# The last stage of a four-layer graph network: overlapped steps, one joined turn for sums and edge sums, norms and stores by chunk

## The chip, the cores and the metric

The kernel runs on one core of one Trainium2 chip. The metric is the device time of one launch, in microseconds (us). Three launches of the kernel before took 26902.59, 26913.0 and 26931.47 us; the median is 26913.0 us.

## What is computed

The reference applies four layers to a graph with 12500 nodes of 64 features and 400000 edges. The fourth layer, with the edge sum taken over the edges that leave a node, is where the change lies:

```python
# h is the normed and rectified x, of 12500 x 64
msg = h[j] + (edge_attr @ We + be)                # 400000 edges, edge_attr of 16 features
agg = segment_sum(msg, i, 12500)
t = (1.0 + eps) * h + agg
out = relu(t @ W1 + b1) @ W2 + b2
out = (out - mean(out)) * rsqrt(var(out) + 1e-5) * gamma + beta     # over the 64 features
x = x + out                                       # the result
```

The edge weights We and their bias be are the same for all edges. So the kernel sums, for each node, the gathered h (64 columns), the number of edges (1 column) and the raw edge attributes (16 columns), and multiplies the last 17 columns by the rows be and We only afterwards.

## The kernel before

All node data lie in SBUF as 98 blocks of 128 nodes: node 128 b + p is on partition p, and block b is 64 columns wide (81 in `acc2`, which holds the sums: 64 of messages, 1 of edges, 16 of attributes). One big SBUF tensor, `arena`, holds every buffer, and one PSUM tensor, `psum`, all eight banks; in the profile nearly all operands therefore carry these two names, and groups are told apart by their lines.

The kernel is a row of stages with a barrier of all engines between them (line 104). Sorting and record writing come first, then a gather layer or a table stage in turn for the first three network layers, then the messages of the fourth layer are scattered into source order (`scatter_messages`), summed per source (`source_sums`, lines 1246 to 1304) and turned into the result by `last_stage` (lines 1310 to 1430). The stages before the last one take most of the time, and the change does not touch them. Within a stage each engine has its own instruction list, in program order, and the engines meet only at semaphores. `peeled` runs step 0 apart and then loops over the other steps. `wait_earlier` is a wait that falls away at zero.

`last_stage` before has three parts.

Loads: SyncE issues nine small loads of weights, biases and eps. TensorE, ScalarE and VectorE wait for all nine.

Steps: 14 steps of 7 blocks. VectorE copies the 17 edge columns out (line 1364) and forms (1 + eps) h + sums (line 1365). TensorE turns both by multiplying them with the identity matrix, block by block, 7 times lines 1410 and 1412. ScalarE copies the turned edge sums from PSUM (line 1389, in two halves of 512 and 384 columns). TensorE multiplies them by the edge weights, added in PSUM to the turned sums (line 1417). VectorE copies that out (line 1370), TensorE multiplies by W1 (line 1423), ScalarE adds b1 and rectifies (line 1394), TensorE multiplies by W2 (line 1428), and VectorE adds b2 and writes the block's output (line 1373). There is one buffer for each of these values, and TensorE's list has a whole step before the next one begins.

Norm and store: when all steps are done, VectorE norms all 98 blocks in passes over 6272 columns each (`layer_norm`, lines 718 to 728; the square root is ScalarE's, line 1398), multiplies by gamma, adds beta, adds x (lines 1378 to 1380), and SyncE then stores the result (lines 1338 and 1339). Each pass waits for the one before.

Of the kernel before, what the change touches and what calls it, by code (L numbers as in the profile page):

```python
# [41 lines left out]
ARENA = 53200  # L42
# [9 lines left out]
MW = D + 1 + FE  # L52
# [66 lines left out]
def build(nc, a, out):  # L119
    ctx = ExitStack()  # L120
    with ctx:
# [51 lines left out]
        source_sums(nc, sem, Buffers(arena, b.at), psum, iotab, blks, acc2, rec2)  # L173
        sem.end_stage()
        last_stage(nc, sem, a, Buffers(arena, b.at), psum, ident, epsc, x, acc, h, acc2, out)


# [1129 lines left out]
            peeled(pe, GROUPS2 // RING2, step)  # L1307


def last_stage(nc, sem, a, b, psum, ident, epsc, x, acc, h, acc2, out):  # L1310

    sq = b.take(NB * D)
    small = [b.take(NB) for _ in range(3)]
    web, w1, w2, b1, b2, gam, bet, ep = b.take(D), b.take(P), b.take(D), b.take(1), b.take(D), b.take(D), b.take(D), b.take(1)
    BL = 7
    steps = NB // BL
    mb, sb, st, ht, ut = (b.take(BL * n) for n in (D, 1 + FE, P, P, P))
    names = ("w", "v", "m", "s", "st", "a", "ht", "u", "ut", "o", "ob", "sum", "std", "x", "out")
    s_w, s_v, s_m, s_s, s_st, s_a, s_ht, s_u, s_ut, s_o, s_ob, s_sum, s_std, s_x, s_out = (sem("z_" + n) for n in names)
    ps_a, ps_s, ps_u, ps_o = (psum[:, 1024 * k:1024 * k + BL * P] for k in range(4))  # L1320
    halves = [(0, 512), (512, BL * P)]
    whole = N // P
    x3 = x.rearrange("p (b f) -> p b f", f=D)

    with nc.Block() as block:
        @block.sync
        def _(sp):
            sp.dma_start(web[0:1, :], a["be"]).then_inc(s_w, 16)
            sp.dma_start(web[1:1 + FE, :], a["we"]).then_inc(s_w, 16)
            sp.wait_ge(s_v, 1)  # L1330
            sp.dma_start(w1[0:D, 0:D], a["w1"]).then_inc(s_w, 16)
            sp.dma_start(w2[0:D, :], a["w2l"]).then_inc(s_w, 16)
            sp.dma_start(b1[0:D, :], a["b1"]).then_inc(s_w, 16)
            for t, n in ((b2, "b2"), (gam, "gamma"), (bet, "beta")):
                sp.dma_start(t, a[n].to_broadcast([P, D])).then_inc(s_w, 16)
            sp.dma_start(ep, a["eps"].to_broadcast([P, 1])).then_inc(s_w, 16)
            sp.wait_ge(s_x, 1)
            sp.dma_start(out[0:whole * P, :].rearrange("(b p) f -> p b f", p=P), x3[:, 0:whole, :]).then_inc(s_out, 16)
            sp.dma_start(out[whole * P:N, :], x3[0:N - whole * P, whole, :]).then_inc(s_out, 16)
            sp.wait_ge(s_out, 32)  # L1340

        @block.vector
        def _(dve):
            v = nc.vector
            chain = [0]

            def link(ins):
                chain[0] += 1
                ins.then_inc(s_v, 1)
                dve.wait_ge(s_v, chain[0])  # L1350

            link(v.memset(w1, 0.0))
            dve.wait_ge(s_w, 16 * 9)
            link(v.tensor_scalar(ep, ep, 1.0, None, ALU.add))
            a3 = acc2.rearrange("p (b f) -> p b f", f=MW)
            h3 = h.rearrange("p (b f) -> p b f", f=D)
            o3 = acc.rearrange("p (b f) -> p b f", f=D)
            bias = b2.rearrange("p (o f) -> p o f", o=1).to_broadcast([P, BL, D])

            def step(i):  # L1360
                at = bass.ds(i * BL, BL)

                wait_earlier(dve, s_s, i)
                v.tensor_copy(sb.rearrange("p (b f) -> p b f", f=1 + FE), a3[:, at, D:MW])
                v.scalar_tensor_tensor(mb.rearrange("p (b f) -> p b f", f=D), h3[:, at, :], ep, a3[:, at, 0:D],  # L1365
                                       ALU.mult, ALU.add).then_inc(s_m, 1)
                dve.wait_ge(s_a, i + 1)
                wait_earlier(dve, s_u, i)
                for c, e in halves:
                    last = v.tensor_copy(ht[0:D, c:e], ps_a[0:D, c:e])  # L1370
                last.then_inc(s_ht, 1)
                dve.wait_ge(s_o, i + 1)
                v.tensor_tensor(o3[:, at, :], ps_o[:, 0:BL * D].rearrange("p (b f) -> p b f", f=D), bias, ALU.add).then_inc(s_ob, 1)
            peeled(dve, steps, step)
            dve.wait_ge(s_ob, steps)
            layer_norm(nc, dve, link, s_sum, s_std, 1, acc, h, sq, small, False)
            wide = lambda t: t.rearrange("p (o f) -> p o f", o=1).to_broadcast([P, NB, D])
            link(v.tensor_tensor(h3, h3, wide(gam), ALU.mult))  # L1378
            link(v.tensor_tensor(h3, h3, wide(bet), ALU.add))  # L1379
            v.tensor_tensor(x, x, h, ALU.add).then_inc(s_x, 1)  # L1380

        @block.scalar
        def _(act):
            act.wait_ge(s_w, 16 * 9)
            def step(i):
                act.wait_ge(s_s, i + 1)
                wait_earlier(act, s_a, i)
                for c, e in halves:
                    last = nc.scalar.copy(st[0:1 + FE, c:e], ps_s[0:1 + FE, c:e])  # L1389
                last.then_inc(s_st, 1)  # L1390
                act.wait_ge(s_u, i + 1)
                wait_earlier(act, s_o, i)
                for c, e in halves:
                    last = nc.scalar.activation(ut[0:D, c:e], ps_u[0:D, c:e], ACT.Relu, bias=b1[0:D, :])  # L1394
                last.then_inc(s_ut, 1)
            peeled(act, steps, step)
            act.wait_ge(s_sum, 1)
            nc.scalar.activation(small[2], small[1], ACT.Sqrt, bias=epsc, scale=1.0 / D).then_inc(s_std, 1)

        @block.tensor  # L1400
        def _(pe):
            pe.wait_ge(s_w, 16 * 9)
            def step(i):
                pe.wait_ge(s_m, i + 1)

                wait_earlier(pe, s_st, i)
                wait_earlier(pe, s_ht, i)

                for k in range(BL):
                    nc.tensor.matmul(ps_s[0:1 + FE, k * P:(k + 1) * P], sb[:, k * (1 + FE):(k + 1) * (1 + FE)], ident,  # L1410
                                     start=True, stop=True)
                    last = nc.tensor.matmul(ps_a[0:D, k * P:(k + 1) * P], mb[:, k * D:(k + 1) * D], ident,  # L1412
                                            start=k % 4 == 0, stop=False, skip_group_check=True)
                last.then_inc(s_s, 1)
                pe.wait_ge(s_st, i + 1)
                for k in range(BL):
                    last = nc.tensor.matmul(ps_a[0:D, k * P:(k + 1) * P], web[0:1 + FE, :], st[0:1 + FE, k * P:(k + 1) * P],  # L1417
                                            start=False, stop=k in (3, BL - 1), skip_group_check=True)
                last.then_inc(s_a, 1)
                pe.wait_ge(s_ht, i + 1)  # L1420
                wait_earlier(pe, s_ut, i)
                for c, e in halves:
                    last = nc.tensor.matmul(ps_u[:, c:e], w1[0:D, :], ht[0:D, c:e], start=True, stop=True)  # L1423
                last.then_inc(s_u, 1)
                pe.wait_ge(s_ut, i + 1)
                wait_earlier(pe, s_ob, i)
                for k in range(BL):
                    last = nc.tensor.matmul(ps_o[:, k * D:(k + 1) * D], ut[0:D, k * P:(k + 1) * P], w2[0:D, :], start=True, stop=True)  # L1428
                last.then_inc(s_o, 1)
            peeled(pe, steps, step)  # L1430

# [39 lines left out]
```

## Time and profile before

| | us |
|---|---|
| median of three launches | 26913.0 |
| span of the profiled execution, first to last instruction | 22991.7 |
| last stage in that span: its steps, line 1410 of step 0 to the start of the last line 1373 | 22607.19 to 22919.06 |
| norm, from the first reduction to the end of the last pass | 22919.72 to 22974.94 |
| store of the result | 22974.97 to 22991.7 |

No time other than its span is recorded for the profiled execution. The launches take 3921.3 us more than this span, and the profile shows nothing of that difference.

In the profile a matmul of two fp32 operands appears as two records (x2), each with a weight load. PE is TensorE's multiplication, PEld its weight load, DVE VectorE, ACT ScalarE, POOL GpSimd, SP SyncE. PEclk is the granted TensorE clock: 1.00 is 2.4 GHz and 0.50 is 1.2 GHz; a value between them is a stretch that has both.

### The profile page before, as it was taken

Reading aid. Unit: us, or ns where it says so; the run is one execution under the profiler, and the core shown is the slowest. Engines: PE = TensorE matmul, PEld = TensorE weight load, DVE = VectorE, ACT = ScalarE, POOL = GpSimd, SP = SyncE. Lnnn points to the kernel's source line nnn. Section 1 sums busy time; section 2 is a strip of 40 time slices with the busy share of each in tenths; the row PEclk is TensorE's granted clock in tenths of the full one; section 3 lists DMA queues with packets and bytes.
Section 4 is the critical chain, followed back from the end, with each engine's and each line's share of the span. In section 5 each row is a group of like instructions: output and inputs, shape, how many; then the busy total and the mean of one; then the engine's idle time right before and its main releaser. Section 6 shows DMA issues by size and latency. Waiting matters only on the chain. (4 is left out here: it accounts for less than half of the span.)

```text
span 22991.7 us, 207917 instructions
## 1 busy us (share of the span) xinstructions
PE 9432.7 (41%) x48147; PEld 7206.5 (31%) x48150; DVE 10159.5 (44%) x25131; ACT 1783.1 (8%) x4849; POOL 15546.8 (68%) x16453
## 2 busy tenths in 40 slices
PE   2777776433333333333333633333332222222366
PEld 1333333233333333333333333333331111111254
DVE  7777777544444443333333432222224333333473
ACT  4000000000000000000000200000001111111100
POOL 2777777777777757777777267777776777777400
PEclk7555555555555555555555655555555555555686
DMA  3333332222222222222222322222223222222462
GB/s 103 99 98 98 99 98 77 69 64 61 61 64 61 64 40 66 61 61 61 61 61 61 83 78 64 61 64 61 61 61 66 83 82 83 83 82 82 133 221 70
DMA packets 1005113, 1785.47 MB, mean 78 GB/s; under 512 B 352294, under 2 KB 461123, under 8 KB 1004534
## 3 DMA queue, kind: packets, MB, share of 16 engines
q1 hardware_dynamic: 484294, 1127.71, 15.7%
q0 software_dynamic: 513696, 654.80, 12.5%
q10 hardware_dynamic: 7056, 2.21, 0.0%
q8 instruction: 24, 0.39, 0.0%
q14 instruction: 43, 0.35, 0.0%
HBM read 1279.37 MB, written 510.79 MB: 78 GB/s over the span
## 5 line engine op out<-in xcount | busy, mean ns | idle before, releaser
L1031 PE MATMUL psum<-arena 128*128 128x64 f32 x19392 | 4447.7, 424 | 7932.5 <-DMA arena<-table,arena 4593.2
L932 POOL DMA_INDIRECT arena<-table,arena x6464 | 6108.0, 945 | 2006.7 <-issue 1927.4
L1031 PEld LDWEIGHTS psum<-arena 128*128 128x128 f32 x19392 | 4227.4, 330 | 8153.0 <-issue 6213.6
L983 DVE TENSOR_TENSOR arena<-arena,psum 128x64 f32 x9696 | 2150.8, 222 | 6335.1 <-PE psum L1031 4421.4
L700 POOL DMA_INDIRECT rec<-arena x3125 | 3003.1, 961 | 1376.6 <-issue 948.7
L1136 POOL DMA_INDIRECT rec<-arena x3232 | 3180.9, 984 | 1093.7 <-issue 970.4
L932 POOL DMA_INDIRECT arena<-ptable,arena x3232 | 3148.0, 974 | 998.1 <-issue 984.7
L477 PE MATMUL psum<-arena 128*128 128x196 bf16 (+1 forms) x4375 | 1378.8, 429 | 1265.0 <-DVE arena L608 1264.9
L1155 DVE TENSOR_TENSOR arena<-psum,arena 128x1024 bf16<-128x1024 f32 x404 | 494.6, 1224 | 2715.2 <-DMA arena<-rec 2715.2
L1203 PE MATMUL psum<-arena 128*128 128x128 bf16 x3232 | 418.2, 311 | 2527.4 <-DVE arena L1155 2527.4
L1203 PEld LDWEIGHTS psum<-arena 128*128 128x128 bf16 x3232 | 312.9, 141 | 2674.0 <-DVE arena L1155 2346.4
L608 DVE TENSOR_TENSOR arena<-psum,arena 128x392 f32<-128x392 f32 x1875 | 918.1, 490 | 362.0 <-PE psum L477 236.7
L477 PEld LDWEIGHTS psum<-arena 128*128 128x128 bf16 x4375 | 367.6, 115 | 2190.5 <-DVE arena L608 1814.9
L962 DVE TENSOR_TENSOR arena<-psum,arena 128x1024 f32<-128x1024 f32 x808 | 984.5, 1219 | 25.6 <-issue 24.0
L989 DVE TENSOR_TENSOR arena<-arena 128x512 f32<-128x512 f32 x404 | 286.6, 710 | 1585.0 <-DMA arena<-ptable,arena 1585.0
L1214 PE MATMUL psum<-arena 128*128 x3232 | 589.7, 363 | 642.5 <-DVE arena L1163 553.3
L1304 PE MATMUL psum<-arena 128*128 128x81 bf16 x10560 | 605.2, 228 | 475.8 <-DVE arena L1272 466.8
L613 DVE TENSOR_REDUCE arena<-arena 128x10 f32<-128x980 f32 x625 | 734.0, 1174 | 21.6
L600 DVE TENSOR_TENSOR arena<-psum,arena 128x980 bf16<-128x980 f32 x625 | 729.4, 1167 | 0.0
L1163 DVE CAST arena<-psum 128x1536 bf16<-128x1536 f32 x404 | 707.3, 1751 | 7.1 <-PE psum L1214 6.9
L1304 PEld LDWEIGHTS psum<-arena 128*128 128x128 bf16 x10560 | 539.2, 116 | 542.0 <-issue 447.6
L788 ACT ACTIVATE arena<-arena 128x98 f32<-128x98 f32 x3 | 1.1, 376 | 8313.7 <-DVE arena L722 8313.7
(194 smaller groups left out, 10126.3 us busy)
## 6 DMA issues: line engine op xcount, KB each, us to landing
arena<-rec SPq DMA_DIRECT2D x303, 1408.0 KB
arena<-rec SPq DMA_DIRECT2D x440, 488.0 KB, 4.4
arena<-in_edge SPq DMA_DIRECT2D x625, 232.0 KB, 2.6
arena<-rec SPq DMA_DIRECT2D x404, 352.0 KB, 3.3
arena<-table,arena POOLq DMA_INDIRECT x6464, 2.4
rec<-arena POOLq DMA_INDIRECT x6357, 2.3
table<-arena SPq DMA_DIRECT2D x196, 512.0 KB
arena<-ptable,arena POOLq DMA_INDIRECT x3232, 2.4
```

Source lines behind the costliest of these rows:

```text
L477: return nc.tensor.matmul(to, identb, one_hots, start=False, stop=False, skip_group_check=True)
L600: v.tensor_tensor(buf[g].rearrange("p (t w) -> p t w", w=NB), numsw, keyw, ALU.is_equal).then_inc(s_hot, 1)
L608: v.tensor_tensor(prod[g][:, 2 * n * WIDE:2 * n * WIDE + w], run[:, 0:w], buf[g][:, 2 * n * WIDE:2 * n * WIDE + w], ALU.mult).then_inc(s_s ...
L613: v.tensor_reduce(posf[:, g * CG * KEYS:(g + 1) * CG * KEYS], prod[g].rearrange("p (t w) -> p t w", w=NB), AX.X, ALU.add).then_inc(s_red, 1)
L700: nc.gpsimd.indirect_dma_start(rec, bass.IndirectOffsetOnAxis(ap=stage[g][:, j:j + 1], axis=0), recs[g][:, j * RW:(j + 1) * RW], None).the ...
L932: nc.gpsimd.indirect_dma_start(rows[q][:, j * D:(j + 1) * D], None, tab, bass.IndirectOffsetOnAxis(ap=idx[:, j, field:field + 1], axis=0)) ...
L962: v.tensor_tensor(ones, iotas, lanes, ALU.is_equal).then_inc(s_hot[q], 1)
L983: v.tensor_tensor(block_sum, block_sum, ps[q % SB][:, j * D:(j + 1) * D], ALU.add).then_inc(s_add[j], 1)
L1031: last = nc.tensor.matmul(ps[q % SB][:, j * D:(j + 1) * D], hot[q % SB][:, j * P:(j + 1) * P], rows[q][:, j * D:(j + 1) * D], start=True, ...
L1136: nc.gpsimd.indirect_dma_start(rec2, bass.IndirectOffsetOnAxis(ap=idx[:, j, R_SLOT:R_SLOT + 1], axis=0), rows[q][:, j * ROW:(j + 1) * ROW] ...
L1203: last = nc.tensor.transpose(ps_t[q % 2][:, j * P:(j + 1) * P], hot[q][:, j * P:(j + 1) * P], identb)
L1304: last = nc.tensor.matmul(ps[q % RING][j // QT], hot[q][:, j * P:(j + 1) * P], rows[q][:, at:at + MW], start=j % QT == 0 and k == 0, stop= ...
```

## The change

Only `last_stage` and two arrays that the host prepares are changed. In the changed stage:

- The 98 blocks form 7 chunks of 14 blocks for VectorE's wide passes, and each chunk is two steps of 7 blocks for TensorE. All loops are written out, so no engine loops in this stage.
- (1 + eps) h + sums is written back into the first 64 of the 81 columns of `acc2`, and one turn per block handles all 81 columns. The copy of the edge columns is gone.
- The edge weights enter through one 81 x 64 matrix, the product of [unit | be, We turned] with W1, built once by one matmul and one copy. The product with the edge weights per block (line 1417) is gone.
- TensorE's list is turn(s), inner(s-1), outer(s-2). The turned values, the rectified ones and the outputs have two buffers each; the inner product has one PSUM buffer.
- ScalarE makes both copies from PSUM, each as one instruction of 896 columns, and also the squares of the norm. VectorE's norm runs by chunk behind the steps.
- GpSimd adds beta to x by chunk, from the loads on.
- SyncE stores each chunk when it is ready.

```diff
-            def step(i):                                    # TensorE
-                ...
-                for k in range(BL):
-                    nc.tensor.matmul(ps_s[0:1 + FE, k * P:(k + 1) * P], sb[:, k * (1 + FE):(k + 1) * (1 + FE)], ident, ...)
-                    last = nc.tensor.matmul(ps_a[0:D, k * P:(k + 1) * P], mb[:, k * D:(k + 1) * D], ident, ...)
-                last.then_inc(s_s, 1)
-                pe.wait_ge(s_st, i + 1)
-                for k in range(BL):
-                    last = nc.tensor.matmul(ps_a[0:D, k * P:(k + 1) * P], web[0:1 + FE, :], st[0:1 + FE, k * P:(k + 1) * P], ...)
-                ...
+            def turn(s):
+                pe.wait_ge(s_mix, s // 2 + 1)
+                wait_earlier(pe, s_ht, s - 1)
+                for j in range(SUB):
+                    n = s * SUB + j
+                    last = nc.tensor.matmul(ps_t[s % 2][:, j * P:(j + 1) * P], acc2[:, n * MW:(n + 1) * MW], ident, start=True, stop=True)
+                last.then_inc(s_t, 1)
+
+            def inner(s):
+                pe.wait_ge(s_ht, s + 1)
+                wait_earlier(pe, s_ut, s)
+                for c, e in halves:
+                    last = nc.tensor.matmul(ps_u[:, c:e], wc[0:KW, :], ht[s % 2][0:KW, c:e], start=True, stop=True)
+                last.then_inc(s_u, 1)
+
+            def outer(s):
+                pe.wait_ge(s_ut, s + 1)
+                wait_earlier(pe, s_ob, s - 1)
+                for j in range(SUB):
+                    last = nc.tensor.matmul(ps_o[s % 2][:, j * D:(j + 1) * D], ut[s % 2][0:D, j * P:(j + 1) * P], w2[0:D, :],
+                                            start=True, stop=True)
+                last.then_inc(s_o, 1)
+
+            pe.wait_ge(s_w, WEIGHTS)
+            nc.tensor.matmul(ps_w, zc[0:D, :], w1[0:D, :], start=True, stop=True).then_inc(s_wp, 1)
+            turn(0)
+            pe.wait_ge(s_wc, 1)
+            for s in range(1, SUBS + 2):
+                if s < SUBS:
+                    turn(s)
+                if s - 1 < SUBS:
+                    inner(s - 1)
+                if s >= 2:
+                    outer(s - 2)
+        # VectorE: seven times (1 + eps) h + sums first, then
+            def centre(k):
+                dve.wait_ge(s_ob, 2 * k + 2)
+                v.tensor_reduce(total[:, blocks(k)], rows_of(o, k, CH), AX.X, ALU.add).then_inc(s_total, 1)
+                dve.wait_ge(s_total, k + 1)
+                v.scalar_tensor_tensor(rows_of(o, k, CH), spread(total, k), -1.0 / D, rows_of(o, k, CH),
+                                       ALU.mult, ALU.add).then_inc(s_mid, 1)
+
+            def spreads(k):
+                dve.wait_ge(s_sq, k + 1)
+                v.tensor_reduce(var[:, blocks(k)], rows_of(sq, k, CH), AX.X, ALU.add).then_inc(s_var, 1)
+
+            def normal(k):
+                ...    # reciprocal, times it, times gamma, plus (x + beta): three passes of 896 columns
+            for s in range(2, 2 * LAST + 9):
+                if s - 2 < SUBS:
+                    take_product(s - 2)
+                if s % 2 == 0 and 0 <= (s - 4) // 2 < CHUNKS:
+                    centre((s - 4) // 2)
+                if s % 2 == 0 and 0 <= (s - 6) // 2 < CHUNKS:
+                    spreads((s - 6) // 2)
+                if s % 2 == 0 and 0 <= (s - 8) // 2 < CHUNKS:
+                    normal((s - 8) // 2)
+        @block.gpsimd
+        def _(pool):
+            pool.wait_ge(s_w, WEIGHTS)
+            for k in range(CHUNKS):
+                nc.gpsimd.tensor_tensor(rows_of(x, k, CH), rows_of(x, k, CH), row(bet, CH), ALU.add).then_inc(s_xb, 1)
```

On ScalarE the list of step s is: the copy of turn(s), the rectifying of inner(s-1), and in odd steps the squares of a chunk and the square root of an earlier one.

## Rows read from the trace of the kernel before

**Rows 1.** The page: the profiled execution's span.

```profile
span 22991.7 us, 207917 instructions
```

**Rows 2.** The chain of waits in one step: start us, us, engine, operand, line, count.

```profile
22607.77 0.62 PE psum L1412 x2
22608.39 0.54 PE psum L1410 x2
...
22616.45 3.25 PE psum L1417 x14
22619.73 1.16 DVE arena L1370 x2
22620.93 3.37 PE psum L1423 x4
...
22625.52 3.26 PE psum L1428 x14
...
22629.54 0.68 DVE arena L1365
...
22630.26 0.61 PE psum L1410 x2
```

**Rows 3.** Timeline, stage's head: start us, us, engine, line, operation, operands, [idle before, releaser].

```profile
22605.98 0.15 DVE L1354 TENSOR_SCALAR arena<-arena 128x1 f32<-128x1 f32 x1 [6.57 <-DMA arena<-in_eps]
```

**Rows 4.** Timeline from the last step to the store.

```profile
22919.06 0.62 DVE L1373 TENSOR_TENSOR arena<-psum,arena 128x448 f32 x1 [8.04 <-PE psum L1428]
22919.72 6.69 DVE L718 TENSOR_REDUCE arena<-arena 128x98 f32<-128x6272 f32 x1
...
22947.27 0.77 DVE L724 RECIPROCAL arena<-arena 128x98 f32<-128x98 f32 x1 [0.44 <-ACT arena L1398]
...
22968.25 6.69 DVE L1380 TENSOR_TENSOR arena<-arena 128x6272 f32<-128x6272 f32 x1
...
22975.41 13.85 SPq L1339 DMA_DIRECT2D result<-arena  x1
```

**Rows 5.** Groups of the last stage: line, engine, operation, shapes, count, busy us, mean ns.

```profile
L1394 ACT ACTIVATE arena<-psum,arena 64x512 f32<-64x512 f32 x14 | 9.6, 684 | 104.2 <-PE psum L1423 104.2
...
L1365 DVE SCALAR_TENSOR_TENSOR arena<-arena 128x448 f32 x13 | 8.9, 685 | 0.0
L1373 DVE TENSOR_TENSOR arena<-psum,arena 128x448 f32 x13 | 8.1, 625 | 104.6 <-PE psum L1428 104.6
L1389 ACT COPY arena<-psum 17x512 f32<-17x512 f32 x14 | 8.1, 577 | 198.9 <-PE psum L1412 198.9
L1394 ACT ACTIVATE arena<-psum,arena 64x384 f32<-64x384 f32 x14 | 7.9, 565 | 0.0
```

**Rows 6.** Timeline of TensorE in a stretch of the last stage at full clock.

```profile
22814.40 0.43 PE L1412 MATMUL psum<-arena 128*64 128x128 f32 x2
...
22814.76 0.39 PE L1410 MATMUL psum<-arena 128*17 128x128 f32 x2
...
22815.08 0.43 PE L1412 MATMUL psum<-arena 128*64 128x128 f32 x2
...
22817.24 1.75 PE L1417 MATMUL psum<-arena 17*64 17x128 f32 x14 [1.04 <-ACT arena L1389]
```

**Rows 7.** Windows: stretch, length, busy of PE, PEld, DVE, ACT, POOL; PEclk; DMA share; GB/s.

```profile
13100.00:13200.00 100.00, 100.00 (x486) 37.32 (x484) 41.61 (x82) 23.74 (x41) 21.66 (x82) 1.00 0.52 210
22400.00:22600.00 200.00, 119.53 (x2098) 106.29 (x2094) 150.25 (x873) 16.69 (x82) 0.00 (x0) 0.82 0.64 202
22600.00:22900.00 300.00, 225.88 (x783) 124.70 (x784) 34.49 (x68) 27.27 (x52) 0.00 (x0) 0.53 0.00 1
22810.00:22814.00 4.00, 4.00 (x16) 1.48 (x16) 0.00 (x0) 0.00 (x0) 0.00 (x0) 0.57 0.00 0
22814.00:22818.00 4.00, 2.96 (x21) 1.67 (x20) 0.00 (x0) 0.95 (x2) 0.00 (x0) 1.00 0.00 0
22818.00:22822.00 4.00, 2.76 (x11) 1.57 (x10) 1.15 (x2) 0.00 (x0) 0.00 (x0) 0.78 0.00 0
```

**Rows 8.** Groups of ScalarE and GpSimd over the whole span.

```profile
L251 ACT ACT_TABLE_LOAD x1 | 1.3, 1283 | 0.6 <-PEq L1460 0.6
L580 ACT ACT_TABLE_LOAD x1 | 1.3, 1283 | 0.0
...
L781 POOL COPY arena<-arena 128x192 bf16 (+1 forms) x196 | 68.4, 349 | 563.0 <-DVEq L861 338.0 <-PE psum L804 224.9 <-issue 0.2
```

More of the change, by code:

```diff
@@ L1307, in _ @@
             peeled(pe, GROUPS2 // RING2, step)
-def last_stage(nc, sem, a, b, psum, ident, epsc, x, acc, h, acc2, out):
[L1312 to L1323, printed above, removed]
+CH = 14
@@ new lines, with rows_of, spread @@
+CHUNKS = NB // CH
+SUB = 7
+SUBS = NB // SUB
+assert CH % SUB == 0 and CHUNKS * CH == NB
+def rows_of(t, k, n, f=D):
+    return t[:, k * n * f:(k + 1) * n * f].rearrange("p (b f) -> p b f", f=f)
+def spread(t, k):
+    return t[:, k * CH:(k + 1) * CH].rearrange("p (b o) -> p b o", o=1).to_broadcast([P, CH, D])
+def last_stage(nc, sem, a, b, psum, ident, epsc, x, acc, h, acc2, out):
+    KW = MW
+    o, sq = acc, b.take(NB * D)
+    total, var, rs = (b.take(NB) for _ in range(3))
+    zc, wc, w1, w2 = b.take(KW), b.take(D), b.take(D), b.take(D)
+    b1, b2, gam, bet, ep = b.take(1), b.take(D), b.take(D), b.take(D), b.take(1)
+    ht, ut = ([b.take(SUB * P) for _ in range(2)] for _ in range(2))
+    assert b.at <= ARENA - NB * D
+    names = ("w", "ep", "zc", "mix", "wp", "wc", "t", "ht", "u", "ut", "o", "ob", "total", "mid", "sq", "var", "std", "rs", "n", "g", "xb", "x", "out")
+    (s_w, s_ep, s_zc, s_mix, s_wp, s_wc, s_t, s_ht, s_u, s_ut, s_o, s_ob, s_total, s_mid, s_sq, s_var, s_std, s_rs, s_n, s_g, s_xb, s_x,
+     s_out) = (sem("z_" + n) for n in names)
+    ps_t = [psum[0:KW, 1024 * k:1024 * k + SUB * P] for k in range(2)]
+    ps_u = psum[0:D, 2048:2048 + SUB * P]
+    ps_o = [psum[:, 3072 + 512 * k:3072 + 512 * k + SUB * D] for k in range(2)]
+    ps_w = psum[0:KW, 3584:3584 + D]
+    halves = [(0, 512), (512, SUB * P)]
+    a3 = acc2.rearrange("p (b f) -> p b f", f=MW)
+    row = lambda t, n: t.rearrange("p (o f) -> p o f", o=1).to_broadcast([P, n, D])
+    blocks = lambda k: slice(k * CH, (k + 1) * CH)
+    LAST = CHUNKS - 1
+    WEIGHTS = 16 * 9
@@ L1327, in _ @@
         def _(sp):
[L1328 to L1331, printed above, removed]
+            sp.dma_start(zc[0:D, D:KW], a["web"]).then_inc(s_w, 16)
+            sp.dma_start(w1[0:D, :], a["w1"]).then_inc(s_w, 16)
+            sp.dma_start(ep, a["eps"].to_broadcast([P, 1])).then_inc(s_w, 16)
+            sp.dma_start(bet, a["beta"].to_broadcast([P, D])).then_inc(s_w, 16)
             sp.dma_start(w2[0:D, :], a["w2l"]).then_inc(s_w, 16)
             sp.dma_start(b1[0:D, :], a["b1"]).then_inc(s_w, 16)
[L1334 to L1340, printed above, removed]
+            sp.dma_start(b2, a["b2"].to_broadcast([P, D])).then_inc(s_w, 16)
+            sp.dma_start(gam, a["gamma"].to_broadcast([P, D])).then_inc(s_w, 16)
+            sp.dma_start(zc[0:D, 0:D], a["unit"]).then_inc(s_w, 16)
+            whole = N // P
+            for k in range(CHUNKS):
+                sp.wait_ge(s_x, k + 1)
+                full = min((k + 1) * CH, whole)
+                sp.dma_start(out[k * CH * P:full * P, :].rearrange("(b p) f -> p b f", p=P),
+                             x[:, k * CH * D:full * D].rearrange("p (b f) -> p b f", f=D)).then_inc(s_out, 16)
+            sp.dma_start(out[whole * P:N, :], x[0:N - whole * P, whole * D:(whole + 1) * D]).then_inc(s_out, 16)
+            sp.wait_ge(s_out, 16 * (CHUNKS + 1))
+        @block.gpsimd
+        def _(pool):
+            pool.wait_ge(s_w, WEIGHTS)
+            for k in range(CHUNKS):
+                nc.gpsimd.tensor_tensor(rows_of(x, k, CH), rows_of(x, k, CH), row(bet, CH), ALU.add).then_inc(s_xb, 1)
         @block.vector
@@ L1374, in _ @@
[L1374 to L1380, printed above, removed]
+            dve.wait_ge(s_w, WEIGHTS)
+            v.tensor_scalar(ep, ep, 1.0, None, ALU.add).then_inc(s_ep, 1)
@@ new lines, in _, with take_product @@
+            dve.wait_ge(s_ep, 1)
+            for k in range(CHUNKS):
+                v.scalar_tensor_tensor(a3[:, blocks(k), 0:D], rows_of(h, k, CH), ep, a3[:, blocks(k), 0:D],
+                                       ALU.mult, ALU.add).then_inc(s_mix, 1)
+                if k == 0:
+                    dve.wait_ge(s_wp, 1)
+                    v.tensor_copy(wc[0:KW, :], ps_w).then_inc(s_wc, 1)
+            def take_product(s):
+                dve.wait_ge(s_o, s + 1)
+                v.tensor_tensor(rows_of(o, s, SUB), rows_of(ps_o[s % 2], 0, SUB), row(b2, SUB), ALU.add).then_inc(s_ob, 1)
@@ new lines, in normal @@
+            def normal(k):
+                dve.wait_ge(s_std, k + 1)
+                v.reciprocal(rs[:, blocks(k)], rs[:, blocks(k)]).then_inc(s_rs, 1)
+                dve.wait_ge(s_rs, k + 1)
+                v.tensor_tensor(rows_of(o, k, CH), rows_of(o, k, CH), spread(rs, k), ALU.mult).then_inc(s_n, 1)
+                dve.wait_ge(s_n, k + 1)
+                v.tensor_tensor(rows_of(o, k, CH), rows_of(o, k, CH), row(gam, CH), ALU.mult).then_inc(s_g, 1)
+                dve.wait_ge(s_xb, k + 1)
+                dve.wait_ge(s_g, k + 1)
+                v.tensor_tensor(rows_of(x, k, CH), rows_of(x, k, CH), rows_of(o, k, CH), ALU.add).then_inc(s_x, 1)
@@ L1385, in step @@
[L1385 to L1395, printed above, removed]
@@ L1396, in _ @@
-            peeled(act, steps, step)
-            act.wait_ge(s_sum, 1)
-            nc.scalar.activation(small[2], small[1], ACT.Sqrt, bias=epsc, scale=1.0 / D).then_inc(s_std, 1)
+            act.wait_ge(s_w, WEIGHTS)
+            for s in range(2 * LAST + 8):
+                if s < SUBS:
+                    act.wait_ge(s_t, s + 1)
+                    wait_earlier(act, s_u, s - 1)
+                    nc.scalar.copy(ht[s % 2][0:KW, :], ps_t[s % 2]).then_inc(s_ht, 1)
+                if 0 <= s - 1 < SUBS:
+                    act.wait_ge(s_u, s)
+                    wait_earlier(act, s_o, s - 2)
+                    nc.scalar.activation(ut[(s - 1) % 2][0:D, :], ps_u, ACT.Relu, bias=b1[0:D, :]).then_inc(s_ut, 1)
+                if s % 2 == 1 and 0 <= (s - 5) // 2 < CHUNKS:
+                    k = (s - 5) // 2
+                    act.wait_ge(s_mid, k + 1)
+                    nc.scalar.activation(rows_of(sq, k, CH), rows_of(o, k, CH), ACT.Square).then_inc(s_sq, 1)
+                if s % 2 == 1 and 0 <= (s - 7) // 2 < CHUNKS:
+                    k = (s - 7) // 2
+                    act.wait_ge(s_var, k + 1)
+                    nc.scalar.activation(rs[:, blocks(k)], var[:, blocks(k)], ACT.Sqrt, bias=epsc, scale=1.0 / D).then_inc(s_std, 1)
```

49 lines of the change are left out of this document (3 added, 46 removed).

## The prediction

> **What bounds the kernel now.** The page gives one number to start from, the span of the profiled execution [rows 1]: 22991.7 us, while the launches take 26913.0 us at the median. I make the sum on the span and carry the microseconds over unchanged; the 3921.3 us that the profile doesn't show are taken as untouched, and two rivals below question that.
>
> The change lies in the last stage alone, so the only views that matter are those of its stretch. The chain of waits comes first [rows 2]. The reader is to see that it passes from engine to engine without a gap and that every piece is on it: turns on PE, a copy on ACT, the edge product on PE (3.25 us), a copy on DVE (1.16), the W1 product (3.37), ACT, the W2 product (3.26), DVE, and only then the next step's turns. One step takes 22630.26 - 22607.19 = 23.1 us where the clock stays low (the first turn of step 0 starts 0.58 us before the first row of the group). All 14 take 22919.06 - 22607.19 = 311.9 us, 22.3 each. Nothing overlaps: ACT waits 198.9 us for the turns and DVE 104.6 us for the W2 product [rows 5]. The timeline of the end comes second [rows 4]: from 22919.72 to 22974.94 DVE alone is at work, 55.2 us, in eight passes of 6272 columns and small ones, and from 22974.97 to 22991.7 the store alone, 16.7 us. So steps + norm + store are 384.5 us, and that is all that the change can take from. The windows come third, for the clock [rows 7].
>
> **The head.** Nine loads before, nine after, on the same queue; DVE's first operation waits for the last of them until 22605.98 [rows 3]. I leave that time. DVE then forms the first chunk's sum. A 448-column pass takes 0.685 us [rows 5] and a 6272-column one 6.69 [rows 4], so 1.03 ns a column and 896 columns take 1.15 us. The first turn begins at 22605.98 + 0.15 + 1.15 + hops = 22607.4, 0.2 later than before. The added product for the joined weights runs on PE beside that pass; its copy on DVE (64 columns, under 0.3 us) lies under turn(0) and turn(1). The other six sums (6.9 us) lie under the first turns. Cost of all this on the path: 0.2 us. If a load landed late, everything would shift by it; bounds -1 to +3 us.
>
> **TensorE after.** Per step of 7 blocks its list has 7 turns of 81 columns, the W1 product in two halves with 81 rows instead of 64, and 7 W2 products.
> - At 1.2 GHz a turn takes 0.54 us with 17 columns and 0.62 with 64 [rows 2], a slope of 0.08/47 per column, so 0.65 with 81: 4.55 us. W1: 3.37. W2: 3.26. Sum 11.2 us, 14 steps 156.5 us. (3.37 and 3.26 contain one drain each that back-to-back groups should hide, so this is the upper side.) What goes is the second turn per block, the edge product, and every wait between the groups.
> - At 2.4 GHz the turns take 0.32 and 0.36 us, from the starts 22814.40, 22814.76 and 22815.08 [rows 6], so 0.375 with 81 columns and 2.6 for seven. The edge product, which at 1.2 GHz costs the same as the W2 product (3.25 against 3.26), took 1.75 [rows 6]; I take that for W2. No W1 product ran at full clock; between half of 3.37 and all of it, I take half, 1.7, since it has the longest streams. Sum 6.1 us, 14 steps 85 us.
>
> Which clock? In the last stage before, PE is busy 225.88 of 300 us and the clock is 0.53 [rows 7]. But it rose, inside a burst of turns: from 22810 to 22814 PE is busy without a pause and the share is 0.57, the next 4 us stand at 1.00, and after the pauses for ACT and DVE it falls again (0.78) [rows 7]. Where PE never pauses, it is at 1.00 for 100 us together, and the stage before the last one has 0.82 at 60% busy [rows 7]. After the change PE should not pause at all, so I take the full clock for nearly all of it, and 5 us for a low start and a dip or two: 90 us.
>
> The Trainium skill speaks against this in "TensorE: Matmul & The Clock Gate", section "Part 4: PE-mode transpose": the full clock is said not to engage for TensorE's transpose mode, which doesn't count as busy in the same way. If turns by an identity matmul fell under it, a third of the list would be dead for the clock and the stage would stay at the cold sum, 156.5 us. The trace disagrees for this form of turn, because the clock rose amid nothing but turns [rows 7]; that they are ordinary matmuls may be why.
>
> **What could make PE pause.** inner(s) needs the copy of turn(s) and the rectified inner(s-1), since that PSUM buffer is single. ACT's copy of 896 columns: 577 ns for 512 columns [rows 5], and by the slope of the rectifying halves (684 - 565)/128 = 0.93 ns a column, 0.93 us; the rectifying is 684 + 384 x 0.93 = 1.04 us. Between inner(s-1) and inner(s) PE has outer(s-2) and turn(s+1), 4.3 us even at full clock, over 1.04 plus hops; the copy has inner(s-1) and outer(s-2) over it. ACT's whole load is 0.93 + 1.04 + half of (squares of 896 columns, about 1.0, and a root of 0.3) = 2.6 us a step of 6.1. Two table loads appear in the whole trace, of 1.28 us, none in this stage although it has copies, rectifying and a root [rows 8]; if squares needed another table, two loads per chunk would add 1.3 us a step, and ACT would still be at 3.9. Price nothing; with both clocks low nothing either.
> DVE per chunk: two takings of 0.625 [rows 5], six passes of 1.15, a reciprocal of 14 columns (0.77 for 98 [rows 4], so at most 0.2): 8.3 us and some hops, 8.9, against two PE steps of 12.1. It is no bound, but it has less room than ACT. outer(s) waits only for the taking of s-2, which DVE does ahead of the long even turns (7.5 us); the next taking is late by about 2 us and is needed a whole step later. Added cost: 0, bounds 0 to 15 us.
> GpSimd's additions of beta: a one-input bf16 copy of 192 columns takes 0.35 us [rows 8]; 896 columns of fp32 with two inputs aren't in the trace, so between 0.35 and, tenfold of that row by columns and inputs and a slower type, 5 us each, 35 us in all. I take 2 us each. The first is wanted by normal(0), some 45 us after the head, and one every 12 us after it; hidden at both ends. Were they to slow DVE, the first sum would be the one that counts: 0 to 2 us.
> The skill's "GPSIMD Engine Reference", section "8. Key points", names that contention, for VectorE instructions with two SBUF inputs, which DVE's seven sums are. By it the sum would be up to 2 us longer; no row here shows GpSimd computing beside such a pass.
>
> **The end after.** When outer(13) ends, DVE has in its list: taking 0.62, centre(6) 2.3, spreads(5) 1.15, normal(4) 3.6, spreads(6) 1.15, normal(5) 3.6, normal(6) 3.6: 16.0 us, and some 22 hops of 0.04 (from the copy of line 1370 to the product of line 1423 [rows 2]), 17 us. Bounds 14 to 22. Then the last store. The whole result took 16.7 us before, and the issue that lasts as long as the bytes go out 13.85 of them [rows 4]; so 2.9 us are fixed, and the last chunk, 13 of 98 blocks, takes 2.9 + 1.8 = 4.7 us. The six other stores (each 2.0 us of bytes by the same row) lie under the steps; SyncE has nothing else in its list.
>
> **Sum.** 22607.4 + 90 + 17 + 4.7 = 22719.1 against 22991.7: 273 us less. 26913.0 - 273 = 26640 us, 1.0% less.
>
> **Rivals.**
> 1. The clock stays at 1.2 GHz. For: inner and outer fill only 81 or 64 of the rows, and in every step before, the clock was low while such products ran (0.53 over the stage [rows 7]). Against: the pauses around them. Then 156.5 us in place of 90: 22785.6, 206 us less, 26707 us.
> 2. DVE is the bound. It decides from 12.1 us per chunk, 36% over my 8.9. For: long chains of dependent passes beside GpSimd. At 14 us per chunk the steps take 98 and the end 17 x 14/8.9 = 27: 18 more, 26658 us.
> 3. The launches stretch what the profile shows. 26913.0/22991.7 = 1.17. If the missing time is spread evenly, the saving is 273 x 1.17 = 320: 26593 us. Against: nothing in the profile shows what the 3921.3 us are.
> 4. Slower. The time around the span grows with the length of the program: the stage is now written out 14 times, where before it was one step and a loop. It cancels the saving from a growth of 273/3921.3 = 7.0% and is told from no change from 8.4%; at 9% it gives 26913 - 273 + 353 = 26993 us. For: the span's 3921.3 us must come from something. Against: the last stage is a small part of the program.
> 5. Between 1 and the forecast: the clock rises in the turns and falls in the products of each step, 120 us of PE, 26670 us.
>
> **Chances.** Forecast 0.52, rival 1 0.20, rival 2 0.08, rival 3 0.08, rival 4 0.02, rival 5 0.10. The range takes in all but rival 4 and the fringes: 26590 to 26722 (rival 3 at the low end, rival 1 with a late load and a long end at the high one). Faster by over 0.2% (54 us, about what a measurement of this kernel can tell from none): 0.97; within it 0.01; slower 0.02.
>
> **What would show it.** Right: in the stretch from 22607 PE busy over 95% and PEclk over 0.9 for 90 us; line groups of turns at 0.375 us per block; DVE busy some 70% of that; one chain of DVE passes of 17 us after the last W2 product; a store of 4.7 us at the end; span 22719. Rival 1: the same, with turns at 0.65 and PEclk 0.5. Rival 2: PE idle before its W2 products, released by DVE. Rival 3: the span as forecast and the launches 320 us shorter. Rival 4: the span shorter and the launches not. The forecast is wrong if the launches save under 200 or over 330 us.

## The result, and the profile after

The changed kernel took 26624.62 us at the median of four launches (26618.64 to 26631.85), the kernel before 26917.02: 292.4 us less, a ratio of 0.9895 with a 95% interval of 0.9881 to 0.9909. The forecast was 26640, in a range of 26590 to 26722.

First a word on the spans. The profile of after has a span of 26630.0 us, within 2 us of its launch. The kernel before, profiled again, had 27083.7 us, also within 2 us of its launch. In a later batch, on another chip, the same kernel took 23009 us. So some batches take 22.7 to 23.0 ms and some 26.6 to 27.1, and the profile with the span of 22991.7 us is one of the first kind, in which the stages before the last one are shorter. The row writes of line 700 show it: from the first to the last they take 3978 us in that profile and 3974 in the changed kernel of the shorter batch, but 4964 and 4859 in the two profiles of 27083.7 and 26630.0 us. The last stage is the same on both, within 1 us. I measure it from the end of the last addition of the stage before (line 1265) to the end of the span:

| kernel | last stage, us |
|---|---|
| before / before again | 393.7 / 394.2 |
| after / after again | 108.4 / 109.1 |

That is 285.3 us less; the launches of one kernel scatter over 13 to 29 us, which covers the other 7.

The chain of waits of after, its columns as in [rows 2], shows the steps:

```profile
26530.18 2.59 DVE arena L1386
...
26532.81 4.72 PE psum L1456 x28
26537.53 1.65 PE psum L1463 x4
26539.19 1.69 PE psum L1456 x14
26540.87 1.65 PE psum L1463 x4
26542.53 1.70 PE psum L1470 x14
...
26601.32 1.72 PE psum L1470 x14
...
26603.06 0.63 DVE arena L1394
...
26610.39 0.55 DVE arena L1394
...
26624.87 1.09 DVE arena L1416
```

Where [rows 2] went from engine to engine, here one engine follows itself: turns (L1456), W1 product (L1463), W2 product (L1470), 5.04 us a step instead of 22.3, with no wait of TensorE between its first turn and the end of its last product. The timeline has that end, 26601.25 + 3.69 = 26604.94, in the row of the last two W2 products together:

```profile
26601.25 3.69 PE L1470 MATMUL psum<-arena 64*128 64x64 f32 x28
```

The windows say at which clock:

```profile
26534.00:26538.00 4.00, 4.00 (x26) 3.55 (x26) 4.00 (x3) 1.33 (x2) 4.00 (x3) 0.78 0.00 0
26538.00:26542.00 4.00, 4.00 (x21) 2.22 (x20) 4.00 (x2) 2.38 (x3) 4.00 (x2) 1.00 0.00 0
...
26602.00:26606.00 4.00, 2.94 (x24) 2.75 (x22) 3.44 (x6) 0.52 (x2) 0.00 (x0) 0.76 0.55 115
```

From 26534 on PE is busy 4.00 of 4 us in all windows but the last, and PEclk is 1.00 in all between the first and the last, against 0.53 in [rows 7]. In the last window it is 1.00 up to 26604 and 0.53 from there to 26604.94, although PE is still busy. The groups of the stage, columns as in [rows 5]:

```profile
L1456 PE MATMUL psum<-arena 128*81 128x128 f32 x196 | 25.8, 287 | 2.3 <-DVE arena L1386 2.3
...
L1386 DVE SCALAR_TENSOR_TENSOR arena<-arena 128x896 f32<-128x896 f32 x7 | 18.0, 2627 | 0.0
L1377 POOL TENSOR_TENSOR arena<-arena 128x896 f32<-128x896 f32 x7 | 17.2, 2498 | 1021.5 <-DMA arena<-in_unit 1021.5
...
L1435 ACT COPY arena<-psum 81x896 f32<-81x896 f32 x14 | 12.6, 902 | 52.5 <-PE psum L1456 52.5
L1394 DVE TENSOR_TENSOR arena<-psum,arena 128x448 f32<-128x448 f32 x14 | 8.7, 623 | 22.3 <-PE psum L1470 22.3
```

From the first turn's group on, PE waits for nothing but the first sum (2.3 us); ACT waits 52.5 us for the turns and DVE 22.3 us for the W2 products. They waited for PE before as well, 198.9 and 104.6 us [rows 5], but there PE in turn stood still while they worked.

### The profile page after: what moved, and what is told of

Read it like the earlier page. It is cut to its first block and busy times, and to the rows that moved or that the text cites. A ratio compares the mean times of both kernels' runs of the same rounds, so it can differ in the third digit from the quotient of the medians.

```text
span 26630.0 us, 206931 instructions
## 1 busy us (share of the span) xinstructions
PE 9281.0 (35%) x47759; PEld 7313.2 (27%) x47760; DVE 10151.5 (38%) x25121; ACT 1702.3 (6%) x4834; POOL 15515.5 (58%) x16460
## 5 line engine op out<-in xcount | busy, mean ns | idle before, releaser
L1031 PE MATMUL psum<-arena 128*128 128x64 f32 x19392 | 4517.0, 407 | 10216.4 <-issue 6992.5
L1031 PEld LDWEIGHTS psum<-arena 128*128 128x128 f32 x19392 | 4370.8, 326 | 10362.9 <-issue 8656.1
L932 POOL DMA_INDIRECT arena<-ptable,arena x3232 | 3090.1, 956 | 2211.6 <-DMA arena<-rec 1053.4
L1189 ACT COPY arena<-psum 128x1024 bf16<-128x1024 bf16 x404 | 408.8, 1012 | 3901.9 <-DMA rec<-arena 2743.7
L958 DVE TENSOR_TENSOR psum<-psum,arena 128x1024 f32<-128x1024 f32 x404 | 497.4, 1231 | 314.7 <-issue 313.0
L1272 DVE TENSOR_SCALAR arena<-arena 128x128 bf16<-128x128 bf16 x3520 | 610.9, 249 | 16.6 <-issue 16.6
```

The lines of the kernel that those rows point to most:

```text
L932: nc.gpsimd.indirect_dma_start(rows[q][:, j * D:(j + 1) * D], None, tab, bass.IndirectOffsetOnAxis(ap=idx[:, j, field:field + 1], axis=0)) ...
L1031: last = nc.tensor.matmul(ps[q % SB][:, j * D:(j + 1) * D], hot[q % SB][:, j * P:(j + 1) * P], rows[q][:, j * D:(j + 1) * D], start=True, ...
```

## The experiments

All of them are read by the length of the last stage, since the stages before it vary from launch to launch by more than most of these edits do. Each length comes from one profile. Two profiles of one kernel differ by 0.5 us (before) and 0.7 us (after). The 0.7 lie in the first fourteen turns, which took 4.72 us in the one and 5.42 in the other, because the clock rose at another moment; differences of under about 1 us are therefore not read.

### The kernel before, once more

> The kernel before, unchanged, for a second profile. The profile of the changed kernel has a span of 26630.0 us, within 2 us of its launch, where the first profile of the kernel before had 22991.7 of 26913. Theory 1: the first profile lost 3921 us of recorded time in the long stages, and nothing lies around the span: the span is now about 26915 us and the last stage (from the last addition of the stage before to the end) is 394 us as before. Theory 2 (rival 3 of the prediction): the launches stretch the work by 1.17; then the span differs from the launch again, or the last stage comes out near 461 us.

The span was 27083.7 us for a launch of 27085.46, and the stage 394.2 us. Theory 1 was right that nothing lies around the span. That records had been lost was wrong: both profiles have 207917 instructions, and there was a batch in which the kernel before took 23009.13 us, so such launches are real. Theory 2 falls, since the stage is 394 us whichever total surrounds it.

### The overlap of the steps undone

```diff
-            for s in range(1, SUBS + 2):
-                if s < SUBS:
-                    turn(s)
-                if s - 1 < SUBS:
-                    inner(s - 1)
-                if s >= 2:
-                    outer(s - 2)
+            for s in range(SUBS):
+                if s:
+                    turn(s)
+                inner(s)
+                outer(s)
```

ScalarE's list is changed to match: copy and rectifying of the same step.

> The overlap of the fourteen steps alone is undone: TensorE's list is turn, inner, outer of one step after the other, and ScalarE's is copy and rectifying of the same step; joined turn, joined weights, norm and stores by chunk stay. The last stage is 108.4 us in the changed kernel and 393.7 before. Theory 1, the overlap is worth little beside the smaller work, and the clock stays full with pauses of 1 us: a step is 1.7 + 0.9 + 1.65 + 1.0 + 1.7 and hops, 7.2 us, the stage 108 + 14 x 2.1 = 138 us. Theory 2, the pauses let the clock fall to 1.2 GHz as in the kernel before: a step is 12.1 us, the stage about 205 us, and the launch some 95 us over the changed kernel (26720).

The stage took 176.4 us, the launch a ratio of 0.9913 (0.9897 to 0.993) to before. It lies between the theories, and the chain of waits says why:

```profile
26699.28 3.18 PE psum L1455 x14
26702.48 0.91 ACT arena L1435
26703.44 1.74 PE psum L1462 x4
26705.20 1.01 ACT arena L1438
26706.25 3.25 PE psum L1469 x14
26709.50 3.19 PE psum L1455 x14
```

One step, 10.2 us. W1's product (L1462) takes 1.74 us, the time it has at 2.4 GHz; the turns (L1455) and W2's product (L1469) take 3.2 each, as at 1.2 GHz. The windows agree, with 0.50 and 0.84 in turn:

```profile
26703.00:26707.00 4.00, 2.47 (x8) 1.22 (x8) 0.00 (x0) 1.39 (x2) 0.00 (x0) 0.84 0.00 0
26707.00:26711.00 4.00, 4.00 (x19) 3.88 (x19) 0.62 (x1) 0.00 (x0) 0.00 (x0) 0.50 0.00 0
```

The clock rises near the end of the turns, after 6.4 us of W2's product and turns without a pause (from 26702.5 on it is 1.00), and falls in the second pause, the one for the rectifying (0.85 in the us from 26705). So undoing the overlap costs 68.0 us, but it was open how much of that is waiting and how much is clock.

### The pauses filled

```diff
+            def fill(s):
+                for _ in range(4):
+                    nc.tensor.matmul(psum[0:KW, 1024 * ((s + 1) % 2) + SUB * P:1024 * ((s + 1) % 2) + 8 * P],
+                                     acc2[:, s * SUB * MW:(s * SUB + 1) * MW], ident, start=True, stop=True)
...
+                fill(s)
                 inner(s)
+                fill(s)
                 outer(s)
```

> As the serial version, but TensorE fills each of its two pauses per step with four more turns of one block (about 1 us at 2.4 GHz) into PSUM that nothing reads. The serial version took 10.23 us a step: the turns and the W2 product at 1.2 GHz, the W1 product at 2.4; its stage was 176.4 us against 108.4. Theory 1, the pauses are what the clock falls for: with them filled it stays at 2.4 GHz and a step is 1.7 + 1.0 + 1.65 + 1.1 + 1.7 = 7.2 us, the stage 134 us; then of the 68 us of the undone overlap 42 were the clock and 26 the waiting itself. Theory 2, the clock follows the kind of work (64 rows of the array in the W2 product), and fills don't change it: 10 us a step or more, the stage 176 us or over.

The stage took 138.6 us, a step 7.27:

```profile
22645.39 1.70 PE psum L1455 x14
...
22647.11 0.91 ACT arena L1435
...
22648.07 1.74 PE psum L1467 x4
...
22649.83 1.01 ACT arena L1438
...
22650.88 1.77 PE psum L1474 x14
22652.65 1.70 PE psum L1455 x14
...
22625.00:22725.00 100.00, 97.62 (x655) 73.61 (x654) 47.06 (x47) 31.70 (x38) 10.65 (x5) 0.99 0.07 15
```

(The last line is a window of the same kernel.) With the chain's order unchanged and work added, the stage is 37.8 us shorter: PEclk is 0.99, and turns and W2's product take 1.7. Theory 1 holds here: with the pauses filled the clock stays up. The fills are turns, so they also change the mix of the work; but the changed kernel has the same mix as the serial version and no fills, and its clock is at 1.00 too. Of the 68.0 us, 37.8 are the clock and 30.2 the waiting.

Pauses don't account for all that the rows show of the clock. In [rows 2] PE is busy with turns for 8 us without a pause, and the edge product behind them still runs at 1.2 GHz; and in the changed kernel the clock fell within the last product. What sets it there is open.

### The norm behind the steps, and one store

```diff
-            for s in range(2, 2 * LAST + 9):
-                ...
+            for s in range(SUBS):
+                take_product(s)
+            for part in (centre, spreads, normal):
+                for k in range(CHUNKS):
+                    part(k)
```

> The norm is moved behind all steps: VectorE takes all fourteen products, then centres all seven chunks, then sums all squares, then normals all; stores by chunk stay. Theory 1, VectorE's passes were hidden under TensorE except those of the last 21 us: the passes take 7 x (2.2 + 1.1 + 3.6) = 48 us behind the steps in place of 21, the stage is 135 us, 27 more. Theory 2, VectorE's passes inside the steps slow TensorE or ScalarE by taking SBUF or PSUM: then the fourteen steps get shorter than 70.2 us and the stage comes out under 130.

The stage took 135.9 us, 27.5 over the changed kernel; the launches a ratio of 0.9904 (0.9887 to 0.992) to before. Of the 27.5 us, 1.2 come from the first fourteen turns, which took 5.91 us this time. Theory 1: a step of TensorE takes 5.04 us with VectorE's passes beside it and without them, so they cost it nothing.

```diff
-            for k in range(CHUNKS):
-                sp.wait_ge(s_x, k + 1)
-                ...
+            sp.wait_ge(s_x, CHUNKS)
+            sp.dma_start(out[0:whole * P, :].rearrange("(b p) f -> p b f", p=P), x[:, 0:whole * D]. ...)
```

> One store of the whole result after the last chunk, as before, in place of seven; all else as in the changed kernel. Theory 1: the end is the 16.7 us of the old store in place of 4.0, the stage 108.4 + 12.7 = 121 us. Theory 2: the early stores disturb the steps (bandwidth of SBUF): then the steps get shorter and the stage is under 119 us.

The stage took 121.3 us, 12.9 more, as theory 1 has it.

### GpSimd's additions after VectorE's sums

```diff
             pool.wait_ge(s_w, WEIGHTS)
+            pool.wait_ge(s_mix, CHUNKS)
```

> GpSimd begins its seven additions of beta only when VectorE has made all seven sums; all else as in the changed kernel. There each sum took 2.6 us and each addition 2.5, side by side. Theory 1, the two engines slow each other: a sum alone takes 1.15 us, the first turn begins 1.45 us earlier and the last stage is about 107 us in place of 108.4; an addition alone takes under 2.4. Theory 2, the sums are slow by themselves, since they write into rows of 81 columns: they stay at 2.6 and the stage at 108.4.

The groups of this kernel:

```profile
L1378 POOL TENSOR_TENSOR arena<-arena 128x896 f32<-128x896 f32 x7 | 12.1, 1770 | 1029.2 <-DVE arena L1387 1029.2
...
L1387 DVE SCALAR_TENSOR_TENSOR arena<-arena 128x896 f32<-128x896 f32 x7 | 7.6, 1143 | 0.0
```

A sum takes 1.14 us instead of 2.63, an addition 1.77 instead of 2.50: theory 1. The Trainium skill's rule ("GPSIMD Engine Reference", section "8. Key points") that GpSimd contends with VectorE instructions of two SBUF inputs is borne out here, by those two pairs. The stage took 108.0 us, 0.4 less and not 1.4. The chain shows where the rest is:

```profile
26639.57 1.16 DVE arena L1387
...
26640.78 5.66 PE psum L1457 x28
```

TensorE began 1.3 us earlier in the stage (9.9 us after its start and not 11.2), but its first fourteen turns took 5.66 us where they had 4.72: PEclk was 0.50 for the first 3.2 us and 0.58 in the next two. In the changed kernel, which began at 26532.81, it was 0.55 from 26534 and 1.00 from 26536. That is not shown to be the price of the earlier start. The changed kernel itself had 5.42 us for these turns in its second profile, and the version with centred weights below, which begins as early as this one, had 5.02 and 4.85.

### Turns of two widths, mixed and apart

The changed kernel's turns take 1.69/7 = 0.241 us at 2.4 GHz with 81 columns. In the kernel before they had 0.32 with 17 and 0.36 with 64 at the same clock [rows 6]. Fewer columns, and slower. Two versions add a turn of the 17 edge columns for each block, into PSUM that nothing reads: in the first, each ahead of the block's own turn, in the second seven of them ahead of the seven.

```diff
                 for j in range(SUB):
                     n = s * SUB + j
+                    nc.tensor.matmul(psum[0:1 + FE, 1024 * (s % 2) + SUB * P:1024 * (s % 2) + 8 * P], acc2[:, n * MW + D:(n + 1) * MW], ident, start=True, stop=True)
                     last = nc.tensor.matmul(ps_t[s % 2][:, j * P:(j + 1) * P], acc2[:, n * MW:(n + 1) * MW], ident, start=True, stop=True)
```

> Each block gets a second turn of its 17 edge columns, ahead of the turn of all 81, into PSUM that nothing reads, as the kernel before alternates turns of 17 and 64 columns. In the changed kernel a turn takes 0.241 us at 2.4 GHz; before, in alternation, 0.32 (17 columns) and 0.36 (64). Theory 1, alternating between turns of two widths exposes the weight loads: the seven pairs take about 4.8 us in place of 1.7, and 14 steps 43 us more, the stage 152 us. Theory 2, the turns before were slow for another reason (the full clock was only just reached, or the open accumulation in PSUM): a pair takes 0.48 us, the stage 108 + 24 = 132 us.

> The same additional turns of 17 columns, but seven of them one after the other and then the seven of 81. Theory 1 (alternation is what costs): 0.24 us each, as one width follows itself, the stage 108 + 24 = 132 us. Theory 2 (narrow turns are slow by themselves): 0.32 us each or more, 140 us, and no different from the mixed order but for the wide turns.

Mixed, the stage took 154.3 us; apart, 132.6. The work is the same, and only its order differs. The timeline of TensorE, first mixed, then apart:

```profile
26700.15 0.39 PE L1456 MATMUL psum<-arena 128*17 128x128 f32 x2
26700.47 0.45 PE L1457 MATMUL psum<-arena 128*81 128x128 f32 x2
26700.85 0.39 PE L1456 MATMUL psum<-arena 128*17 128x128 f32 x2
```

```profile
26699.81 1.70 PE L1456 MATMUL psum<-arena 128*17 128x128 f32 x14
26701.45 1.76 PE L1459 MATMUL psum<-arena 128*81 128x128 f32 x14
26703.13 1.72 PE L1466 MATMUL psum<-arena 81*64 81x512 f32 x4
```

From start to start a pair takes 0.70 us mixed, and 0.234 + 0.24 apart, where 17 columns cost as much as 81; PEclk is 1.00 in both (26690 to 26750, and 26670 to 26750). So alternation is what costs, as theory 1 has it in both. Where the turns write is not it: the last three wide turns of a step write to the same half of the step's PSUM columns as the narrow ones (512 to 1023), the first four to the other half, and all pairs take 0.70. Theory 1's reason, that weight loads are exposed, is not shown: the weight loads are busy 0.33 us per pair mixed and 0.42 apart.

The same on the kernel before, one line:

```diff
                 for k in range(BL):
                     nc.tensor.matmul(ps_s[...], sb[...], ident, start=True, stop=True)
+                for k in range(BL):
                     last = nc.tensor.matmul(ps_a[...], mb[...], ident, ...)
```

> The kernel before with one edit: its seven turns of 17 columns come one after the other and then the seven of 64, in place of pairs. A pair took 1.16 us at 1.2 GHz; in the serial version a turn that follows turns of its own width takes 0.457 at that clock. Theory 1, alternation is what made them slow: seven pairs take 6.4 us in place of 8.1, the last stage 24 us less than 394, about 370. Theory 2, the turns before were slow for what they write (an open accumulation in PSUM): under 5 us are saved.

The stage took 332.2 us, 61.5 less, where 24 were expected. Theory 1 was right that alternation is the cost, but too small, because the clock came on top:

```profile
22750.15 3.17 PE psum L1410 x14
22753.32 2.96 PE psum L1413 x14
...
22757.30 1.76 PE psum L1418 x14
...
22769.76 3.17 PE psum L1410 x14
22772.93 1.72 PE psum L1413 x14
```

Seven turns of 17 columns take 3.17 us at 1.2 GHz, and those of 64 between 1.7 and 3.0, since in most steps the clock is up during them or just after. The edge product (here L1418) then finds it high and takes 1.76 us in place of the 3.25 of [rows 2]. It does so in all 14 steps; before, the clock had risen during the edge product or ahead of it in 5 of 14. From 22620 to 22880 the granted clock was 0.66, against 0.53. That the regrouped turns raise the clock more often is shown; why they do so when 8.1 us of mixed turns, also without a pause, mostly did not, is open.

### A version that is faster than both

W2 and b2 are centred over their columns once, beside the first turns, so the products come out with mean zero; the pass that sums them and the pass that subtracts go, and the rest of the norm moves up. Beta is late, as above.

```diff
+                    v.tensor_reduce(tw[0:D, :], w2[0:D, :], AX.X, ALU.add).then_inc(s_c2, 1)
+                    v.tensor_reduce(tb, b2, AX.X, ALU.add).then_inc(s_c2, 1)
+                    dve.wait_ge(s_c2, 2)
+                    v.scalar_tensor_tensor(w2[0:D, :], tw[0:D, :].to_broadcast([D, D]), -1.0 / D, w2[0:D, :], ALU.mult, ALU.add).then_inc(s_c2, 1)
+                    v.scalar_tensor_tensor(b2, tb.to_broadcast([P, D]), -1.0 / D, b2, ALU.mult, ALU.add).then_inc(s_c2, 1)
...
-                    centre((s - 4) // 2)
```

> W2 and b2 are centred over their columns once, on VectorE, so that the products come out centred, and the two passes per chunk that centre them go; squares, sums of squares and normals move up by two steps; beta is added after the sums. Theory 1, the end is VectorE's list behind the last W2 product, 21.2 us in the changed kernel: it becomes 0.6 + 1.0 + 1.1 + 3.6 + 3.6 = 10 us, the head 1.4 us shorter, the stage 108.4 - 12.6 = 96 us. Theory 2, the end is set by ScalarE's squares and roots, which now stand in the chain: over 102 us.

> The changed kernel, unchanged, beside the version with centred weights on one chip. Its stage is 108.4 us again and the launch 1.06% under the kernel before.

> The version with centred W2 and b2 and late beta. Its stage was 98.4 us in its first run. Theory 1, nothing outside the stage changes: 98.4 again, the launch 10 us (0.04%) under the changed kernel, which five rounds may just tell apart. Theory 2, the other stages vary by more than that from launch to launch, and the launches can't tell the two.

The stage took 98.4 and 98.2 us, against 108.4 and 109.1. In its first batch the launches had a ratio of 0.9889 (0.9873 to 0.9906) to before. In the second the launches took 22712.77 us (22710.32 to 22716.23) against 22727.64 for the changed kernel (22727.16 to 22731.04) on the same chip, with 23009.13 for the kernel before: ratios of 0.9872 (0.9855 to 0.9888) and 0.9879 (0.9862 to 0.9895). No launch of the one overlaps the other's, though the intervals of the ratios do; 14.9 us apart, of which the stage has 10.9. The expected 96 us were missed by 2.4, all of it at the end: from the last W2 product (over at 26745.71 in the timeline) to the last pass (26758.18) are 12.5 us and not 10. ScalarE's squares are in the chain for 0.96 us, as the expectation had them. What it had left out is that VectorE's list has normal(4) before the taking of the last product, which so begins 2.6 us after that product:

```profile
26744.13 0.62 DVE arena L1402
...
26747.26 1.09 DVE arena L1424
26748.35 0.55 DVE arena L1402
26748.92 0.96 ACT arena L1451
```

## Why the prediction was right

**The overlap and the clock: right.** The clock was the largest doubt, with 0.20 for rival 1. It was at 1.00 from about 3 us after the first turn into the last product, which also rules out rival 5. The forecast's reason, that it is the pauses that keep it low, is what the filled version shows for the serial order; that it is not the whole of the matter is said there. The rule of the Trainium skill that was weighed ("TensorE: Matmul & The Clock Gate", section "Part 4: PE-mode transpose") speaks of the transpose mode and did not decide here: the clock rose within the first fourteen turns by the identity.

**TensorE's 90 us: the size was off.** It took 72.1, from 26532.81 to 26604.94. The W1 and W2 products were nearly as forecast (1.65 and 1.70 against 1.7 and 1.75). The mis-sized term is the turn: 0.375 us per block was extended from [rows 6] by its columns, but these rows hold mixed widths, and mixing is what they are slow for. It is 0.241, 0.93 us less per step, 13 in all; the low clock cost 1.3 us at the start and 0.2 at the end, of the 5 set aside.

**The end, 17 us: too short.** It was 21.0, from 26604.94 to 26625.96. I had VectorE idle when outer(13) ends. But in the last two steps TensorE has no turns left, so outer(13) follows outer(12) in 1.7 us, while VectorE has centre(5), spreads(4) and normal(3) between the two takings, which begin at 26603.06 and 26610.39 in the chain above, 7.3 us apart.

**The head: 1.4 us too short.** The first sum took 2.6 us, not 1.15, beside GpSimd; it lay in the bounds given. The store took 4.0 us, not 4.7. On the stage these make -17.9 + 4.0 + 1.4 - 0.7, and 0.4 for later loads: -12.8 against the forecast's 121.1 (22719.1 less the 22598.0 at which the stage begins), which gives the 108.4 measured to within rounding. The total is nearer than its largest term: 17.9 us too much for TensorE and 5.1 too little elsewhere cancel in part, and that is luck.

**The span.** That 3921.3 us lie outside the span was wrong. Carrying the microseconds over unchanged was right all the same, since the last stage is equally long in both kinds of batch.

**Rivals.** DVE was not the bound: it works 8.0 us per chunk against 10.1 of TensorE, closer than the 8.9 against 12.1 foreseen, because TensorE is faster. Rivals 3 and 4 fall with the time around the span, which does not exist: where the whole kernel takes 23009 us, the change saved 281.5 us, and 292.4 where it takes 26917, 1.04 times as much and not 1.17. (Rival 4's bound of 8.4% comes out as 8.3: 273 + 54 of 3921.3.)

**Where the 285 us came from.** By the experiments: overlap of the steps 68.0 (clock 37.8, waiting 30.2), norm by chunk 27.5, early stores 12.9. Taken as if they add up, these leave 177 us. Most of it is the serial step getting shorter, from 22.3 to 10.2 us, 169 us in 14 steps: joined turns at 3.2 us for 8.1, no edge copy and product, W1's product at full clock, and VectorE's sums out of the chain. These parts were not taken away one by one, so their shares are open. In the kernel before, 61.5 us could be had by the order of the turns alone.

## What to carry to other kernels

When one engine's burst ends in a hand-over, price the pause twice: the wait, and the clock that the next burst runs at. A fill that does nothing useful can pay: here it took 37.8 us off the serial version. Where small matmuls with different numbers of weight columns alternate, group them by width before changing anything else. And when a pipeline drains, work through each list once more with the missing work left out: the last steps have other lengths than the steady ones.

## What was not expected of the hardware

Two turns of different widths in alternation take 0.70 us, the same two in runs of seven 0.47. GpSimd and VectorE, each with two SBUF inputs, slow each other from 1.14 to 2.63 and from 1.77 to 2.50 us per 896 columns; one after the other they would take 2.9 us a pair, so side by side is still a little faster (2.6), but not for the one that is waited for. TensorE's clock can stay at 1.2 GHz through 8 us of turns without a pause, and can fall within a product. And the same program takes 22.7 or 26.6 ms, by the batch, with the last stage equal to within 1 us; the indirect row writes of line 700 are one of the stages that differ.
